# Weighted values of two groups of heads in one PSUM bank, an earlier start of batch 1, and indirect DMAs with pauses between them

## The reference

```python
x = x + tanh(g_xattn[0]) * xattn(layernorm(x), ctx, ctx, Wq, Wk, Wv, Wo)
x = x + tanh(g_ffn[0]) * ffn(layernorm(x), router_w, w1, b1, w2, b2)

# xattn: 16 heads of width 8
scores = einsum('bhne,bhme->bhnm', qh, kh) * 0.125
att = softmax(scores, axis=-1)
out_h = einsum('bhnm,bhme->bhne', att, vh)
concat = out_h.transpose(0, 2, 1, 3).reshape(B, N, H * Dh)   # then @ Wo.T
# ffn: 8 experts with a hidden width of 512, the best 2 of each token, weights made to sum to 1
output = output + cw[:, e:e + 1] * out_e
```

## Time and profile before

| | |
|---|---|
| median of 3 timed runs | 1393.27 us (1391.37 to 1396.01) |
| the profiled execution | 1404.85 us, its span 1402.8 us |
| mean granted TensorE clock | 0.969 |
| PE busy | 1328.3 us (95%) |
| DVE busy | 1172.8 us (84%) |
| ACT busy | 1101.0 us (78%) |
| POOL busy | 549.6 us (39%) |
| chain that ended last | PE 85%, DVE 9%, issue 2%, ACT 1%, DMA 1% |

### The profile page before, as it was taken

The page is one execution under the profiler, slowest core; times in us unless marked ns, Lnnn a source line. Parts: engine busy times, 40 slices in busy tenths (PEclk is TensorE's granted clock), DMA queues, the critical chain, the costliest instruction groups (busy, mean ns, idle before and its releaser), DMA issues.

```text
span 1402.8 us, 37968 instructions
## 1 busy us (share of the span) xinstructions
PE 1328.3 (95%) x13936; PEld 646.2 (46%) x13936; DVE 1172.8 (84%) x2302; ACT 1101.0 (78%) x2202; POOL 549.6 (39%) x1213
## 2 busy tenths in 40 slices
PE   4689999999999999999999999999999999998992
PEld 2233444444444444444444444444444433587882
DVE  6687899999999999999999999999999998354444
ACT  1368788888898989898988888888888888764551
POOL 1231526262625353535353535344444312144442
PEclk7699999999999999999999999999999999999996
DMA  3422121212121212121212122122221200375665
GB/s 89 150 64 78 32 70 48 70 44 74 41 76 37 67 46 65 48 63 50 63 51 63 53 59 58 55 60 58 60 57 35 58 29 2 119 235 182 205 205 198
DMA packets 65556, 109.15 MB, mean 78 GB/s; under 512 B 13452, under 2 KB 36364, under 8 KB 65228
## 3 DMA queue, kind: packets, MB, share of 16 engines
q1 hardware_dynamic: 56716, 92.46, 22.4%
q0 software_dynamic: 4544, 9.45, 2.1%
q10 hardware_dynamic: 4112, 4.83, 1.0%
HBM read 48.81 MB, written 14.64 MB: 45 GB/s over the span
## 4 chain that ended last, share of the span: by engine, by line
PE 85%; DVE 9%; issue 2%; ACT 1%; DMA 1%; ACTq 1%; POOL 0%; another core or an unknown queue 0%; POOLq 0%; DVEq 0%; SPq 0%
PE pv L768 30%; PE st L725 15%; PE mxp L747 15%; DVE mx L1465 8%; PE st L992 5%; PE mxp L1002 5%; PE st L836 4%; PE st L827 4%; PE st L847 2%; PE st L799 1%; DVE x_sb L1648 1%; PE st L870 1%; PE st L811 1%; ACT arena L1031 1%; PE mxp L968 1%
## 5 line engine op out<-in xcount | busy, mean ns | idle before, releaser
L1465 DVE TENSOR_REDUCE mx<-mxp 128x2 f32<-128x804 f32 x1024 | 986.2, 988 | 86.3 <-PE mxp L747 72.3
L1031 ACT ACTIVATE arena<-st 128x512 f32<-128x512 f32 (+1 forms) x1664 | 897.2, 594 | 121.1 <-PE st L725 106.5
L768 PE MATMUL pv<-arena 128*32 128x256 f32 x6656 | 536.5, 394 | 0.8 <-ACT pv_sb L1038 0.7
L747 PE MATMUL mxp<-kpack,qpack 48*128 48x402 bf16 x2048 | 452.1, 343 | 26.0 <-DVE mx L1465 12.5
L725 PE MATMUL st<-qpack,kpack 51*128 51x256 bf16 (+1 forms) x3328 | 454.0, 274 | 10.6 <-issue 9.9
L725 PEld LDWEIGHTS st<-qpack,kpack 51*128 51x128 bf16 (+1 forms) x3328 | 205.6, 96 | 214.2 <-ACT arena L1031 108.5
L747 PEld LDWEIGHTS mxp<-kpack,qpack 48*128 48x128 bf16 x2048 | 137.6, 94 | 167.3 <-DVE mx L1465 87.8
L768 PEld LDWEIGHTS pv<-arena 128*32 128x32 f32 x6656 | 131.9, 108 | 178.0 <-issue 87.2
L614 POOL CAST mxs<-nmx 128x8 bf16<-128x8 f32 x64 | 12.2, 191 | 323.6 <-DVE nmx L1473 323.5
L1171 ACT ACTIVATE arena<-st,bias 128x256 f32<-128x256 f32 x156 | 73.4, 474 | 62.6 <-PE st L992 42.7
L655 POOL DMA_INDIRECT results<-ysb,idx x78 | 74.7, 958 | 103.0 <-DVE ysb L1597 90.9
(11 more groups left out here) (183 smaller groups left out, 999.1 us busy)
## 6 DMA issues: line engine op xcount, KB each, us to landing
kpack<-ksp SPq DMA_DIRECT2D x762, 50.0 KB
arena<-in_ctxT SPq DMA_DIRECT2D x15, 800.5 KB, 4.5
arena<-in_w1T SPq DMA_DIRECT2D x39, 256.0 KB
arena<-in_w2T SPq DMA_DIRECT2D x39, 256.0 KB
qpack<-qsp SPq DMA_DIRECT2D x186, 32.0 KB
xblk<-rows SPq DMA_DIRECT2D x39, 132.0 KB
rows<-in_pads SPq DMA_DIRECT2D x8, 264.0 KB
qpack<-mxT SPq DMA_DIRECT2D x128, 3.0 KB
```

The lines of the kernel that those rows point to most:

```text
L747: eng.matmul(mxp[pair % MX_BUFS][:, rg, 0:WIN], qpack[rows, b % 2, g * JJ + jj, t * P:(t + 1) * P], kpack[rows, b % 2, g * JJ + jj, WSTART ...
L768: ins = eng.matmul(pv[32 * j:32 * j + 32, 0:N], vaug[0:n, b % 2, kt, VC * h:VC * h + 32], pt[0:n, (2 * u + rg) % PT_BUFS, jj * N:(jj + 1) ...
L1031: eng.activation(pt[0:n, c % PT_BUFS, :], ring[bank_of["S", u, p]][0:n, :], ACT.Exp, scale=SCALE).then_inc(s_exp, 1)
L1465: eng.tensor_reduce(mx[:, tj, w, :], mxp[windows_done % MX_BUFS][:, :, 0:WIN], AX.X, ALU.max).then_inc(s_red, 1)
```

## The change

**Values.** `vaug` gets 18 columns for a head: nine zeros, the eight values, the one. A group with even number reads its 32 columns from the values on (`at` = 18h + 9), one with odd number from the zeros on, so that its results go to rows 9 to 17 of each head's stretch of pv while those of the even group stay in rows 0 to 8. pv gathers over both groups (26 tiles); `copy_weighted`, `turn_heads` and `divide` then handle two groups at once, 32 times in the program instead of 64, at r = 5 and 35. The order of the heads in `conc` changes, and the rows of Wo with it.

**Front.** SHORT is 5, so 23 windows go ahead of the scores. x rows, queries and values of batch 1 are made there, between windows; its keys are made at r = 7, 9, 10, 11 and packed from r = 14 on. SP loads context 1 before the second group's keys, packs batch 1's queries there too, and takes one of ScalarE's packs.

**x.** One load of batches 2 to 15 on ScalarE becomes one for each batch on SP.

**Indirect DMAs.** The last three row writes of batch 14 wait for units 40, 42 and 44 of batch 15. The second write of expert block i waits for the first layer of block i + 2 (s_hp at 4(i + 3)). The four row writes of batch 15 come behind blocks 9, 12, 15 and 18.

```diff
-VW = VC * (H - 1) + 32
+VP = 2 * VC
+VW = VP * (H - 1) + 32
+TWOS = NG // 2
+COPIES = B * TWOS
-HEADS_AT, TURN_AT, PLACE_AT = {5: 0, 15: 1, 35: 2, 41: 3}, {8: 1, 22: 2, 34: 3, 47: 4}, {9: 1, 23: 2, 35: 3, 48: 4}
+HEADS_AT = {5: 0, 35: 1}
+TURN_AT, PLACE_AT = {8: 1, 22: 2, 34: 3, 47: 4}, {9: 1, 23: 2, 35: 3, 48: 4}
-X1_AT, Q1_AT = 4, 6
-FIRST_K_AT = {10: 0, 12: 1, 16: 2, 18: 3}
+X1_AHEAD, Q1_AHEAD, V1_AHEAD = 1, 2, 8
+FIRST_K_AT = {7: 0, 9: 1, 10: 2, 11: 3}
-LAST_ROWS_AT = 9
-LEAD, SHORT = 28, 9
+ROWS_AT, LAST_ROWS_AT = {1: 40, 2: 42, 3: 44}, {9: 0, 12: 1, 15: 2, 18: 3}
+LEAD, SHORT = 28, 5
...
+            def load_rows(b):
+                if b < B:
+                    eng.dma_start(x_sb[:, b * NT:(b + 1) * NT, :], xs[:, b, :, :]).then_inc(s_x, 16)
...
                     elif r == 35:
                         pack_keys(b + 1, 3)
+                        load_rows(b + 3)
                         load_context(b + 1)
...
                 for j in range(SJ):
                     eng.wait_ge(s_ysb, SJ * i + j + 1)
+                    if j > 0:
+                        eng.wait_ge(s_hp, min(HC * (i + 3), CHUNKS))
...
             for part in range(1, 2 * NT):
+                eng.wait_ge(s_pv, (B - 1) * UNITS + ROWS_AT[part])
                 write_rows(B - 2, part, s_sc)
             for i in range(NBK):
                 write_block(i)
-                if LAST_ROWS_AT <= i < LAST_ROWS_AT + 2 * NT:
-                    write_rows(B - 1, i - LAST_ROWS_AT, s_scl)
+                if i in LAST_ROWS_AT:
+                    write_rows(B - 1, LAST_ROWS_AT[i], s_scl)
...
+                if u == 0:
+                    eng.wait_ge(s_vone, 3)
-                if kt == 0 and u > 0:
-                    eng.wait_ge(s_pvs, b * NG + g)
+                first, last = g % 2 == 0 and kt == 0, g % 2 == 1 and kt == KT - 1
+                if first and u > 0:
+                    eng.wait_ge(s_pvs, (b * NG + g) // 2)
...
-                        vaug[0:n, b % 2, kt, VC * h:VC * h + 32],
+                        pv[32 * j:32 * j + 32, 0:N], vaug[0:n, b % 2, kt, at:at + 32],
-                        start=(kt == 0), stop=(kt == KT - 1), tile_position=(0, 32 * j))
+                        start=first, stop=last, tile_position=(0, 32 * j))
...
-                if n == 3:
+                if n == 0:
                     values(0, NV - 1)
-                if n == NMX + 1:
+                elif n == X1_AHEAD:
+                    turn_rows("X", 1)
+                elif n == Q1_AHEAD:
+                    queries(1)
+                elif V1_AHEAD <= n < V1_AHEAD + VCH[0][1]:
+                    values(1, 0, [n - V1_AHEAD])
+                elif n == NMX + 1:
                     turn_maxima(0)
+                elif n > NMX + 1 and n - NMX - 1 < NV:
+                    values(1, n - NMX - 1)
...
-            eng.dma_start(x_sb[:, 2 * NT:TILES, :].rearrange("p (b t) d -> p b t d", t=NT), xs[:, 2:B, :, :]
-                          ).then_inc(s_x, 16)
...
-                conc[:, :, g, :, :], fin[:, :, 0:DH].rearrange("p (t j) e -> p t j e", t=NT),
+                    conc[:, :, :, 2 * two:2 * two + 2, :].rearrange("p t j g e -> p (t j) g e"),
+                    fin[:, :, :, 0:DH], rden[:, :, :].unsqueeze(3).to_broadcast([P, NT * HG, 2, DH]),
...
+            for n in range(5):
+                norm_step("X", 1, n)
             eng.memset(kone[:, :], 1.0).then_inc(s_kone, 1)
...
+            eng.memset(vparts[:, :, :, 0:VC], 0.0).then_inc(s_vone, 1)
```

More of the change, by code:

```diff
@@ L133, in prepared @@
         return "K", b + 1, keys_at(b)[r]
-    if b + 1 < B and r in V_AT:
+    if 0 < b < B - 1 and r in V_AT:
         return "V", b + 1, V_AT[r]
@@ L155, in ring_banks @@
         take("V", 0, c)
+    take("X", 1)
+    take("Q", 1)
+    take("V", 1, 0)
     take("M", 0)
+    for c in range(1, NV):
+        take("V", 1, c)
     for u in range(B * UNITS):
@@ L162, in ring_banks @@
             take("M", b * NG + TURN_AT[r])
-        if r in HEADS_AT and b * NG + HEADS_AT[r] > 0:
-            take("H", b * NG + HEADS_AT[r] - 1)
+        if r in HEADS_AT and b * TWOS + HEADS_AT[r] > 0:
+            take("H", b * TWOS + HEADS_AT[r] - 1)
         if prepared(b, r):
@@ L393, in first_packs @@
             eng.wait_ge(s_q3, 1)
-            for part in range(PARTS):
+            for part in range(PARTS - rg):
                 pack_query_rows(eng, 0, part, rg)
@@ L828, in keys, with values @@
                            start=True, stop=True).then_inc(s_kp, 1)
-            def values(b, c):
+            def values(b, c, some=None):
                 i = bank_of["V", b, c]
-                eng.wait_ge(*freed[i])
                 t0, tn = VCH[c]
-                for t in range(tn):
+                some = range(tn) if some is None else some
+                if 0 in some:
+                    eng.wait_ge(*freed[i])
+                    if b == 1 and c == 0:
+                        eng.wait_ge(s_ctx[1], 16)
+                for t in some:
                     n = key_rows(t0 + t)
@@ L934, in _ @@
                         keys(b + 1, keys_at(b)[r])
-                    elif r in V_AT:
+                    elif b > 0 and r in V_AT:
                         values(b + 1, V_AT[r])
@@ L1117, in _ @@
             eng.activation(id_bf[:, :], id_sb[:, :], ACT.Copy).then_inc(s_idb, 1)
+            copy_rows(1)
+            first_queries(1)
+            copy_values(1, 0)
             copy_maxima(0)
-            eng.dma_start(x_sb[:, 2 * NT:TILES, :].rearrange("p (b t) d -> p b t d", t=NT), xs[:, 2:B, :, :]
-                          ).then_inc(s_x, 16)
+            for c in range(1, NV):
+                copy_values(1, c)
             for u in range(B * UNITS):
@@ L1124, in _ @@
                 exponentials(u, 1)
-                if u > KT and u % KT == LAG - 1:
-                    copy_weighted(u // KT - 1)
+                if u > 2 * KT and u % (2 * KT) == LAG - 1:
+                    copy_weighted(u // (2 * KT) - 1)
                 if r in TURN_AT and b * NG + TURN_AT[r] < GROUPS:
@@ L1532, in _ @@
                 eng.memset(rank[:, ex:ex + 1], float(NE - ex)).then_inc(s_order, 1)
+            eng.memset(vparts[:, :, :, 0:VC], 0.0).then_inc(s_vone, 1)
+            eng.memset(vaug[:, :, :, VP * H:VW].rearrange("p k t w -> p (k t) w"), 0.0).then_inc(s_vone, 1)
+            eng.wait_ge(s_order, NE)
             for n in range(issued(0, 0)):
                 maximum(*divmod(n, NMX))
-            for n in range(5):
-                norm_step("X", 1, n)
-            eng.wait_ge(s_order, NE)
             for u in range(B * UNITS):
```

123 lines of the change are left out of this document (56 added, 67 removed).

## The result

| | before | after |
|---|---|---|
| first comparison, median | 1393.44 us (1391.37 to 1396.01, 4 runs) | 1376.75 us (1376.51 to 1377.35, 4 runs) |
| ratio, 95% interval | | 0.9879 (0.9864 to 0.9893) |
| repeated later | 1406.35 us (1402.63 to 1409.29, 17 runs) | 1380.27 us (1379.53 to 1380.45, 5 runs) |
| ratio there | | 0.9812 (0.9799 to 0.9824) |

The change makes the kernel faster by 1.2%: 16.7 us, where 30 were forecast, and 1376.75 us lies outside the range of 1350 to 1374. In the repetition it was 26.1 us, because the kernel before was 12.9 us slower there and the changed one 3.5 us. That difference is part of what follows.

The account below looks back on a forecast made before the run. TensorE was taken to bound the batches and experts, with VectorE close behind. Terms 11.1 + 1 + 17.9 = 30.0 us off 1393.3 gave 1363 us in timed runs; range 1350 to 1374 for 8 in 10.

Parts of the forecast that it names:

- Pairs of groups: Batches 1 to 15: 30 removed pairs of transposes at 0.37 us save TensorE 11.1 us, plus 1 us of copy waits.
- Since all three engines lose at the same places, TensorE's gain should arrive whole: At the removed turns TensorE, VectorE and ScalarE all lose work, so the full 11.1 us was counted.
- Rival C: Less comes through: ScalarE paces the tiles (1374 us), or batch 1's maxima still meet the context load (1376 us); chance 0.14.
- Front and batch 0: Start of the kernel through batch 0: earlier scores, fewer windows left and TensorE's stands gone, 17.9 us, bounds 5 and 24.
- First scores at about 46: End of the front: first scores start at about 46 us instead of 46.78, 0.8 us earlier, bounds 0 and 3.
- about 39: Front: time in us of the first maxima's turn, behind which five windows and 5 us of values were counted.
- full clock there: A sign: between 60 and 140 us TensorE runs at full clock, with no stand over 1 us.
- SP's queue: 14 more x loads of about 0.45 us issue at tile 35, where nothing of that batch waits: 0.
- Pauses: Breaking up runs of indirect DMAs: about 10 us less in the profiled execution, 0 in timed runs, bounds 0 and 10.
- I take it that the timed runs don't have them: Timed runs, 11.6 us shorter than the profiled execution, were taken to lack its two slow places, at the experts and before.
- Rival B: The common standstill is in timed runs too and goes away, 10 us more: 1353 us; chance 0.25.
- It fits: 0: Block 23's load after the late fourth row write needs 7 us against 10 available: cost 0, bound 3.

Follow-up runs that it names:

- pair_only: Kernel before with only the two groups in one bank (turns of heads at tiles 5 and 35): 1399.81 us against 1405.72, ratio 0.9958.
- the short reductions: Both kernels with VectorE's window reductions over 322 of 402 columns: kernel before 1391.23 us, changed kernel 1359.04 us.
- front_only: Kernel before with only the new front, batch 1's earlier keys and x loaded batch by batch: 1391.12 us, ratio 0.9891.
- experiment 6: Changed kernel with the work between the first windows spread, 1379.39 us, or with one load of x on ScalarE, 1379.52 us.
- experiment 1: Parts by themselves; for the pauses: kernel before with only them 1399.78 us, ratio 0.9958; changed kernel without them 1385.7 us, ratio 0.9864.
- no_pauses: Changed kernel without the pauses between indirect DMAs: 1385.7 us, ratio 0.9864 against the kernel before.
- after_again: Changed kernel, nothing altered, run and traced again on the second chip beside the kernel before: 1380.27 us.
- before_short: Kernel before with VectorE's window reductions over 322 of 402 columns: 1391.23 us, ratio 0.9882.
- row_pauses_only: Kernel before with only the row writes spread (batch 14's at tiles 40, 42, 44, batch 15's behind blocks 9, 12, 15, 18): 1403.25 us, ratio 0.9982.
- block_pause_only: Kernel before with only each second block write waiting for the first layer of block i + 2: 1402.44 us, ratio 0.9967.
- rows_earlier: Changed kernel with the last row writes behind blocks 9, 11, 13 and 15 instead of 9, 12, 15 and 18: 1378.96 us, ratio 0.9817.

## Why the prediction was wrong

**Pairs of groups.** The step "Since all three engines lose at the same places, TensorE's gain should arrive whole" failed. At the two places where a turn was removed (tiles 15 and 41), it had lain over a wait of the next window for VectorE. With it gone, the window arrives earlier and waits 0.22 us. VectorE loses its divides there as well, but it is then busy with windows, not divides. Measured: 0.33 us a batch instead of 0.74, 5.9 us in all instead of 12.1 (11.1 and 1); shown by `pair_only`, and the reason by the short reductions. Rival C, which gave 1374 or 1376 us, came nearest to the measured 1376.75 by luck: it named ScalarE, let the whole 11.1 us stay away with a period of 71.8, and in its second form kept the waits for the context load, which are gone.

**Front and batch 0.** Right in kind: both stands are gone and batch 0 ends earlier. Batch 1's first weighted values are at 129.98 us, where about 124 were forecast, and batch 0's result is turned at 139.29 us instead of

```profile
152.47 0.44 PE L857 MATMUL st<-id_sb,conc 128*128 128x128 f32 x2
```

(the kernel before), 13.2 us less where 17.9 were forecast; `front_only` gives 14.6 in all. Two terms were mis-sized. "First scores at about 46" came out as 48.38, since the turn at "about 39" came at 41.39. I had laid the new work behind the turn and forgotten what stands ahead of it. There VectorE paces TensorE's windows at 0.90 us each (30.91 - 30.01), and with a value tile between them they follow each other at 1.17 us (32.08 - 30.91). And I took "full clock there" between 60 and 140, while 79 to 87 us run at 0.79, 1.7 us of work (0.21 x 8). The two are 2.4 + 1.7 = 4.1 of the 4.7 missing. They may not add up in this way: in experiment 6, 1.3 us of the first were won back and nothing was left of them at batch 0's end.

**SP's queue** at 0: right (`front_only`, period unchanged).

**Pauses.** The bounds 0 and 10 were right, the choice of 0 for timed runs was not, on the chips where it could be tested: 5.4 to 5.9 us (experiment 1). The step that failed is "I take it that the timed runs don't have them": it drew a cause from one difference of 11.6 us between one execution and three runs. The later runs show that difference between two levels of the same kernel, 1393 and 1406 us. Rival B's argument, a run of indirect DMAs beside both places, was the better one. By the rule that I cited there (the Trainium skill, "DMA: Bandwidth & Descriptors", SWDGE vs HWDGE vs iDMA: queues of different kinds take turns in a DMA engine) the pauses would bring nothing; the traces with and without them say otherwise. Why the engines stop beside such a run was not tried and stays open. Their price: "It fits: 0" failed by 1.1 to 1.4 us (block 22 takes 5.0 to 5.3 us), since the sum counted the tokens' way and not the weights', which SP issues behind them.

**The sum.** Where the parts could be told apart: 5.9 + 14.6 + 5.9 = 26.4, against 12.1 + 17.9 + 0 = 30. That this is near 30 is luck as well: the 5.9 us of the pauses, forecast as 0, make up for much of what the pair and the front lack (6.2 and 3.3). In the first comparison it is 16.7. There the kernel before is 13 us and the changed one 3.5 us below their later times, so the difference is 9.4 us smaller. It is the size of what the pauses bring in a trace (some 156 to 152 us for the blocks, and 67.2 us in `no_pauses` against 63.0 in `after_again` from batch 15's first weighted values to the first block), which would fit the forecast's 0 there; no run of that level was traced, so that is argued and not shown. With the 20.0 us of `no_pauses` and the late block 23, 18.6 would then be left for the first comparison, and 16.7 were measured; the last 2 us stay open.

## What to carry to other kernels

A transfer of work off the bounding engine is worth what is left after its next wait: before counting "n instructions by their duration", look in the timeline whether the instruction behind them would find its buffer free, above all where a second engine is as full as VectorE here (93.5%). A stop of all engines at once in a trace counts for timed runs until a trace without it exists, and long runs of indirect DMAs beside it are its first suspect; a few waits that break them up cost at most the 1.4 us of a late block here. And an earlier start of a stage is no gain until its end moves.

## What the hardware showed that I had not expected

- TensorE, VectorE and ScalarE stop together for 3.4 to 3.6 us around GpSimd's sixth indirect DMA in a row, 1.26 us apart, in each of seven traces with such a run (the kernel before three times, `pair_only`, `front_only`, `no_pauses`, `before_short`). Behind a run of five they stop together for 1.1 us (`row_pauses_only`, 1292.9 to 1294.0). Of the runs of four, those of `block_pause_only` and `rows_earlier` have TensorE stand 1.2 and 1.3 us, and that of the changed kernel at 1253 us has no stop. What decides is not shown.
- Each measurement of the kernel before after the first lies near 1406 us, 0.9% above it, on two chips; the changed kernel moves by 0.2 to 0.3%. A difference between two kernels can depend on the chip or the hour by as much as the effect of one edit.
- 1.3 us of earlier scores were followed by a lower mean clock (0.57 instead of 0.79 over the same 8 us), and both kernels start the same tile's weighted values at 89.15 us.
